# The bias of the hidden layer as three bfloat16 parts, and the loads of early results five tiles later in SyncE's order

## The reference, cut to what matters

```python
logits = xt @ Wr + br                                  # xt: all 8192 tokens
probs, idx = jax.lax.top_k(softmax(logits), 2)         # each token goes to 2 of 8 experts
h = jnp.einsum('td,edf->etf', xt, W1) + b1[:, None, :] # b1: 8 x 512, D=128, F=512
h = _layernorm(relu(h), g1, be1)
y = _layernorm(relu(jnp.einsum('etf,efd->etd', h, W2) + b2[:, None, :]), g2, be2)
x = x + gb * (gate @ y)                                # the two results of a token, weighted
```

## Time and profile before

| | us |
|---|---|
| median of 3 runs | 517.81 (517.48 to 517.86) |
| the profiled execution | 519.68 |
| its span, first to last instruction | 517.6 |
| TensorE busy in the span | 493.6 (95%) |
| VectorE, ScalarE, GpSimd busy | 441.0, 420.0, 365.3 |
| TensorE's granted clock, mean | 0.99 |

### The profile page before, as it was taken

The page is one execution under the profiler, slowest core; times in us unless marked ns, Lnnn a source line. Parts: engine busy times, 40 slices in busy tenths (PEclk is TensorE's granted clock), DMA queues, the critical chain, the costliest instruction groups (busy, mean ns, idle before and its releaser), DMA issues.

```text
span 517.6 us, 14784 instructions
## 1 busy us (share of the span) xinstructions
PE 493.6 (95%) x3101; PEld 393.0 (76%) x3101; DVE 441.0 (85%) x2217; ACT 420.0 (81%) x1148; POOL 365.3 (71%) x483
## 2 busy tenths in 40 slices
PE   7989999999986999999998899999999999999996
PEld 6446665655544799989897789999999989899962
DVE  5778999998887699888887799988989999889893
ACT  5669888978764678888886788899999889999883
POOL 1003666666767778888888878888888888888870
PEclk9999999999997899999999999999999999999999
DMA  6980111145111779867616885666577577667555
GB/s 167 310 233 16 48 47 48 43 134 111 52 46 53 146 166 178 186 200 187 156 52 152 191 224 145 188 198 188 156 200 195 157 193 206 153 184 213 163 164 162
DMA packets 79786, 77.78 MB, mean 150 GB/s; under 512 B 11150, under 2 KB 72745, under 8 KB 79702
## 3 DMA queue, kind: packets, MB, share of 16 engines
q1 hardware_dynamic: 71286, 59.92, 47.4%
q0 software_dynamic: 8416, 16.93, 9.1%
HBM read 54.65 MB, written 22.59 MB: 149 GB/s over the span
## 4 chain that ended last, share of the span: by engine, by line
PE 42%; issue 8%; POOL 6%; DVE 1%; DMA 1%; POOLq 0%; ACT 0%; SPq 0%; DVEq 0%; ACTq 0%
PE bank L1673 15%; PE bank L1570 7%; PE bank L1563 4%; PE bank L1565 4%; PE bank L1564 4%; PE bank L1562 4%; POOL expert_rows L646 3%; PE bank L1554 2%; POOL xi L662 2%; POOL y L662 1%; PE bank L1507 1%; DMA hrow<-expert_rows 1%; PE bank L1686 1%; PE bank L1695 1%; POOL expert_results L674 0%
## 5 line engine op out<-in xcount | busy, mean ns | idle before, releaser
L646 POOL DMA_INDIRECT expert_rows<-rows_ring,slot x128 | 123.1, 962 | 96.1 <-issue 78.6
L674 POOL DMA_INDIRECT expert_results<-y,target x119 | 123.0, 1033 | 31.2 <-issue 26.7
L1673 PE MATMUL bank<-W,h2T 128*128 x720 | 95.5, 276 | 0.8 <-ACT h2T L773 0.3
L1673 PEld LDWEIGHTS bank<-W,h2T 128*128 128x128 f32 x720 | 87.7, 192 | 9.2 <-issue 1.6
L870 ACT ACTIVATE v<-wmod 128x128 f32<-128x128 f32 x135 | 41.9, 311 | 42.3 <-DVE vg L1373 39.2
L1362 DVE SCALAR_TENSOR_TENSOR wmod<-bank,rse,shifts 128x128 f32<-128x128 f32 x119 | 41.6, 350 | 32.9 <-PE bank L1673 25.0
L1562 PE MATMUL bank<-b_parts,onesr 128*128 x135 | 65.1, 482 | 0.7 <-DVE h3lo L1140 0.7
L758 ACT ACTIVATE n<-X,nm,rs 128x128 f32<-128x128 f32 x128 | 54.1, 485 | 8.1 <-DVE nm L1307 8.1
L1145 DVE BATCH_NORM_STATS2 stf<-h1T 128x6 f32<-128x512 f32 x90 | 59.3, 659 | 0.0
L1563 PE MATMUL bank<-W1hi,h3hi 128*128 x135 | 54.1, 401 | 0.0
L1570 PE MATMUL bank<-ident_wr,h1T 128*128 128x128 f32 x360 | 54.0, 273 | 0.0
(11 more groups left out here) (250 smaller groups left out, 1245.7 us busy)
## 6 DMA issues: line engine op xcount, KB each, us to landing
shifts<-expert_shifts SPq DMA_DIRECT2D x119, 192.0 KB, 4.2
hrow<-expert_rows SPq DMA_DIRECT2D x135, 65.0 KB
xi<-expert_results SPq DMA_DIRECT2D x12, 512.0 KB, 6.0
out_x<-X SPq DMA_DIRECT2D x15, 256.0 KB
X<-in_L_attn_x SPq DMA_DIRECT2D x7, 512.0 KB, 7.4
W1lo<-in_L_ffn_W SPq DMA_DIRECT2D x4, 512.0 KB, 6.8
expert_rows<-rows_ring,slot POOLq DMA_INDIRECT x128
expert_results<-y,target POOLq DMA_INDIRECT x119
```

The source lines that it names most:

```text
L646: nc.gpsimd.indirect_dma_start(out=rows_d, out_offset=bass.IndirectOffsetOnAxis(ap=slot[q][:, n // TOPK, n % TOPK:n % TOPK + 1], axis=0), ...
L674: nc.gpsimd.indirect_dma_start(out=results_d, out_offset=bass.IndirectOffsetOnAxis(ap=target[i % TARGETS][:], axis=0), in_=y[k], in_offset ...
L1673: ins = mm(acc, rT[(s - 4) % DEPTH][:, ch * P:(ch + 1) * P], W2[:, bass.ds(e4 * CF + ch, 1), :], start=(ch == 0), stop=(ch == CF - 1))
```

## The change

b1 is split in three bfloat16 parts (`b1_split`), which SyncE copies to the first three rows of a bfloat16 `b1_parts`; the product that adds them takes the bfloat16 `ones` that the kernel has already. The zero filling becomes four copies of the same size, `onesr` goes. ScalarE rounds the first part at the end of its step 0 and the second at the end of its step 1; VectorE subtracts at step 1 as before and once more at step 2. In SyncE's loop, `LOADED_AT` puts `load_early(b)` at i = piece_tile(b, 0) + 6 (59, 66, 74, 82, 89, 97, 105, 113, 120, 128) where it was + 1; batch 10 stays at 131.

```diff
-        b1_parts = sb("b1_parts", [P, E, F], F32R)
-        onesr = sb("onesr", [P, P], F32R)
+        b1_rest = third_rT[0:E, :].bitcast(F32)
+        b1_split = sb("b1_split", [E, 3, F], BF16)
+        b1_parts = sb("b1_parts", [P, E, F], BF16)
...
-            sp.dma_start(b1_parts[0:1, :, :].bitcast(F32), b1hi.bitcast(F32)).then_inc(b1_stored, 16)
-            sp.dma_start(b1_parts[1:2, :, :].bitcast(F32), b1lo[:].bitcast(F32)).then_inc(b1_stored, 16)
+            for n in range(3):
+                sp.dma_start(b1_parts[n:n + 1, :, :], b1_split[:, n, :]).then_inc(b1_stored, 16)
...
-            LOADED_AT = {piece_tile(b, 0) + 1: b for b in range(EARLY)}
+            LOADED_AT = {min(piece_tile(b, 0) + 6, EXPERT_TILES - 4): b for b in range(EARLY)}
...
-            def split_b1():
+            def first_b1_part():
                 act.wait_ge(gains_loaded, 80)
-                act.wait_ge(dve_setup, SETUP_PADDING)
-                nc.scalar.activation(b1hi, b1f[:], ACT.Copy).then_inc(act_setup, 1)
-                nc.scalar.activation(onesr[:], onesf[:], ACT.Copy).then_inc(act_setup, 1)
+                nc.scalar.activation(b1_split[:, 0, :], b1f[:], ACT.Copy).then_inc(act_setup, 1)
+
+            def second_b1_part():
+                act.wait_ge(dve_setup, SETUP_REST)
+                nc.scalar.activation(b1_split[:, 1, :], b1_rest, ACT.Copy).then_inc(act_setup, 1)
...
+            def third_b1_part():
+                dve.wait_ge(act_setup, 4)
+                dve.wait_ge(dve_setup, SETUP_REST)
+                mark(vec.tensor_tensor(b1_split[:, 2, :], b1_rest, b1_split[:, 1, :], ALU.subtract))
...
-                mm(h, onesr[:], b1_parts[:, bass.ds(e, 1), :], start=True, stop=False)
+                mm(h, ones[:], b1_parts[:, bass.ds(e, 1), :], start=True, stop=False)
```

More of the change, by code:

```diff
@@ L117, in adaln_ssm_moe_kernel @@
         third_rT = sb("third_rT", [P, F], F32R)
-        b1hi = third_rT[0:E, :]
-        b1_parts = sb("b1_parts", [P, E, F], F32R)
-        onesr = sb("onesr", [P, P], F32R)
+        b1_rest = third_rT[0:E, :].bitcast(F32)
+        b1_split = sb("b1_split", [E, 3, F], BF16)
+        b1_parts = sb("b1_parts", [P, E, F], BF16)
         onesf = sb("onesf", [P, P])
@@ L143, in adaln_ssm_moe_kernel @@
         b1f = spare_gb[0][0:E, :]
-        b1lo = spare_gb[1][0:E, :]
         assert L == F
@@ L460, in _ @@
             sp.wait_ge(dve_setup, SETUP_END)
-            sp.wait_ge(act_setup, 3)
-            sp.dma_start(b1_parts[0:1, :, :].bitcast(F32), b1hi.bitcast(F32)).then_inc(b1_stored, 16)
-            sp.dma_start(b1_parts[1:2, :, :].bitcast(F32), b1lo[:].bitcast(F32)).then_inc(b1_stored, 16)
+            sp.wait_ge(act_setup, 4)
+            for n in range(3):
+                sp.dma_start(b1_parts[n:n + 1, :, :], b1_split[:, n, :]).then_inc(b1_stored, 16)
             sp.wait_ge(dve_setup, SETUP_PADDING)
@@ L511, in load_shifts @@
                 if i == SLOTS:
-                    sp.wait_ge(b1_stored, 32)
+                    sp.wait_ge(b1_stored, 48)
                 if last_user(i) is not None:
@@ L745, in _ @@
             act.wait_ge(dve_setup, SETUP_PADDING)
-            for e in range(E):
-                ins = nc.scalar.activation(b1_parts[:, e, :], padding[:, TAGS:TAGS + 1].broadcast_to([P, F]), ACT.Copy)
+            for n in range(E // 2):
+                ins = nc.scalar.activation(b1_parts[:, 2 * n:2 * n + 2, :].bitcast(F32).rearrange("p e f -> p (e f)"),
+                                           padding[:, TAGS:TAGS + 1].broadcast_to([P, F]), ACT.Copy)
             ins.then_inc(act_setup, 1)
-            def split_b1():
+            def first_b1_part():
                 act.wait_ge(gains_loaded, 80)
-                act.wait_ge(dve_setup, SETUP_PADDING)
-                nc.scalar.activation(b1hi, b1f[:], ACT.Copy).then_inc(act_setup, 1)
-                nc.scalar.activation(onesr[:], onesf[:], ACT.Copy).then_inc(act_setup, 1)
+                nc.scalar.activation(b1_split[:, 0, :], b1f[:], ACT.Copy).then_inc(act_setup, 1)
+            def second_b1_part():
+                act.wait_ge(dve_setup, SETUP_REST)
+                nc.scalar.activation(b1_split[:, 1, :], b1_rest, ACT.Copy).then_inc(act_setup, 1)
             def normalise(b, dst, x_tiles, rs_, nm_, pieces):
@@ L823, in mixer_step @@
                     normalise(s - 1, n2[1 - q], 0, rs[q], nm[q], range(J // 2, J)).then_inc(n2_ready, 1)
-                if isinstance(s, int) and s == 0:
-                    split_b1()
+                if s == 0:
+                    first_b1_part()
+                if s == 1:
+                    second_b1_part()
             run(mixer_step, FIRST1)
@@ L975, in gains_setup @@
                 dve.wait_ge(act_setup, 3)
-                mark(vec.tensor_tensor(b1lo[:], b1f[:], b1hi, ALU.subtract))
+                mark(vec.tensor_tensor(b1_rest, b1f[:], b1_split[:, 0, :], ALU.subtract))
+                assert done[0] == SETUP_REST
+            def third_b1_part():
+                dve.wait_ge(act_setup, 4)
+                dve.wait_ge(dve_setup, SETUP_REST)
+                mark(vec.tensor_tensor(b1_split[:, 2, :], b1_rest, b1_split[:, 1, :], ALU.subtract))
                 assert done[0] == SETUP_END
@@ L1167, in mixer_step @@
                     gains_setup()
+                if s == 2:
+                    third_b1_part()
                 if on(s - SPLIT_FROM - 1, E):
@@ L1576, in mixer_step @@
                     pe.wait_ge(w1lo_ready, E)
-                    pe.wait_ge(b1_stored, 32)
+                    pe.wait_ge(b1_stored, 48)
                     pe.wait_ge(table_ready, 1)
@@ L1710, in _ @@
                 total_of(b)
-SETUP_PADDING, SETUP_CT, SETUP_MOD, SETUP_GB, SETUP_MIX, SETUP_SUMS, SETUP_END = 2, 3, 4, 8, 12, 13, 14
+SETUP_PADDING, SETUP_CT, SETUP_MOD, SETUP_GB, SETUP_MIX, SETUP_SUMS, SETUP_REST, SETUP_END = 2, 3, 4, 8, 12, 13, 14, 15
 _INS = ['L0_attn_x', 'L0_attn_Win', 'L0_attn_bin_', 'L0_attn_Bp', 'L0_attn_Cp', 'L0_attn_Dp', 'L0_attn_Wout',
```

## The result

The changed kernel takes 590.36 us (median of 4 runs, 588.39 to 593.05), the kernel before beside it 517.64: a ratio of 1.1396, 95% interval 1.1363 to 1.143. The forecast was 590.0. The profiled execution of after took 592.14 with a span of 590.0, against 519.68 and 517.6 before.

The account below looks back on a forecast made before the run. TensorE was taken to bound the second stage. Late loads 55.1, clock 18.0, bias product -1.4 and setup 0.5 sum to +72.2 on 517.81, giving 590.0 us; the forecast's own range was 580 to 597, the wider one 571 to 602.

Parts of the forecast that it names:

- The bound and the late loads: Second stage: TensorE sets the time; loads of batches 0 to 9 come too late and stall it, +55.1 us together.
- a landing of 4 us in the quiet queue: Sign of being wrong: late loads landing in 4 us instead of 6.1, which would take 20 us off.
- behind `h3lo`: Expected sign in the profile after: TensorE waits 5 us behind `h3lo` at the late batches.
- Away goes: Batch 0: SyncE's wait for 39 stored results, which makes tile 55's rows late, disappears; nothing added to the sum.
- The clock: TensorE's granted clock falls behind each of ten stalls, at 1.8 us each: +18.0 us, bounds 0 and 25.5.
- the two rows that the 1.8 was taken from: Two clock falls in the trace before, near 158 and 170 us, costing TensorE 2.55 and 1.7 us.
- Rival 1: TensorE stalls at the late loads but its clock stays up: 572 us; chance 0.10.
- The product with b1: Bias product in bfloat16 is 18 ns shorter over the 79 tiles from 56 on: -1.4 us.
- Rival 4: The bias product gains all of 80 ns, -6.3 us instead of -1.4, on top of the stalls: 585 us; chance 0.05.
- Setup: First stage: an extra copy of half a microsecond on ScalarE before L778 is on the path: +0.5 us (0 to 0.6).
- Rival 2: Stalls feed on each other through slower products, slow landings and costlier clock falls: 601 to 602 us; chance 0.10.
- Rival 3: The moved load is still early enough, so only the other edits count: 516.1 us; chance 0.05.

Follow-up runs that it names:

- run 9: Changed kernel with the relu of the hidden product moved ahead of ScalarE's waiting copy in the ten stalling steps: 588.04 us, ratio 1.1359.
- run 5: Changed kernel with 18 needless TensorE products ahead of the hidden product in the ten stalling tiles, when every kernel was slower: ratio 1.1074.
- run 11: Changed kernel with 18 needless TensorE products ahead of the hidden product in the ten stalling tiles, repeated later: 580.37 us, ratio 1.1187.
- run 3: Changed kernel with load_early at piece + 3 in place of + 6: 519.95 us, ratio 1.0028.
- run 6: Changed kernel, loads still at + 6, with SHIFT_LAG 7 in place of 6 (shifts asked for one tile later in SyncE's order): ratio 1.0791.
- run 1: Kernel before with only the late loads (piece + 6), its bias product left in float32r: 590.24 us, ratio 1.1393.
- run 2: Changed kernel with load_early back at piece + 1, so only the bias edits are left: 517.29 us, ratio 0.9991.
- run 12: The changed kernel itself, run again as a reference beside later runs: 589.4 us, ratio 1.1374.
- run 8: Changed kernel with only batch 5 loaded at piece + 6, all others at + 1: ratio 1.0172; tiles 54 to 134 take 194.95 us.
- run 4: Changed kernel with load_early at piece + 4 in place of + 6: 535.08 us, ratio 1.0331.
- run 7: Changed kernel with load_early back at piece + 1 and SHIFT_LAG 7 in place of 6, when every kernel was slower: ratio 1.0037.
- run 10: Changed kernel with load_early back at piece + 1 and SHIFT_LAG 7 in place of 6, repeated later: 517.17 us, ratio 0.9981.

## Why the prediction was right, step by step

**The bound and the late loads.** Right. The load stands behind the shifts of its own step, goes out 0.39 us behind them (350.51, 350.90), and ScalarE waits at L850 ten times. Of the sum of 55.1, measured 52.7. Two errors in it nearly cancel:
- The landing takes 5.2 us at the median (4.6 to 5.7) instead of 6.1, 9 us less over ten. That the load is quicker because the kernel's other transfers pause in a stall was not tested. The prediction named this as a way to be wrong ("a landing of 4 us in the quiet queue").
- From the copy's start to TensorE it is 1.30 us and not 0.95: the relu behind `h3hi` was missed, +3.5 over ten by the difference, 2.7 by run 9. The sum followed `h3lo` alone. Of the 0.35, 0.27 is the relu (run 9); the other 0.08 is the estimate of signals and issue, which was that much too short. The wait of TensorE "behind `h3lo`" that was to show it reads as one for L772.

The rest, some 3 us, is at batch 0 (8.6 us, forecast 7.3) and at batch 6 (6.7, forecast at most 6.15), where the load took 6.2 us and not 5.2. At batch 0 the load goes out at 301.23, 0.9 later than forecast, which the short landing makes up: the stalled tile starts at 307.35, as forecast. The 1.3 us by which its stall is longer are no loss, since tile 54 starts 1.3 us earlier than before; 0.8 of them are the wait ahead of tile 54, which is gone. That is the point **Away goes** of the prediction, which added nothing, and rightly.

**The clock.** Forecast +18.0, measured 22.0, within the bounds of 0 and 25.5. It fell at all ten places and cost 1.4 to 2.8 us each, 2.2 on average, between the two rows that the 1.8 was taken from. Runs 5 and 11 show that it is TensorE's pause that does it. By the warning of the Trainium skill ("TensorE: Matmul & The Clock Gate", "HAM oscillation") this is paid in every round, and the trace agrees. The mean clock is 0.93 and not the 0.96 that was named as a sign: it is low for part of the pauses too, where it costs nothing. Rival 1 (clock up, 572) is out by this. A rule by the length of the pause alone doesn't come out of the runs: from tile 54 on no pause up to 2.2 us was followed by a fall (1.95 in run 11, 2.09 in run 3, 2.22 in run 6), each from 3.1 us on was, and between them both happened (a fall at 2.35 and 2.44, none at 3.01 and 3.03). The forecast was safe, because its pauses are over 4 us.

**The product with b1.** Forecast -1.4, measured -1.1 (14 ns for each of 80 tiles instead of 18). The row is 379 ns and not 377, and the matching float32r product 395. Rival 4, -6.3, is out: the weight load is half as long (98 ns for 190) and the beat doesn't show it, as the rows have it under the last turn (at tile 95 of after it runs from 438.74 to 438.84, the four turns until 439.01).

**Setup.** Forecast +0.5. Where it arises the forecast is right. From ScalarE's first `xi` (L778 before, L781 now) to that of its step 2 there are 16.90 us in the traces of before and of run 1, which has the old setup, and 17.42 in all twelve with the new one. But in six of these twelve (after and runs 2, 5, 6, 9 and 12) the clock fell right behind, and the next step was 2.1 to 2.2 us late instead of 0.5. In after (windows of 1 us, columns as in the earlier trace rows):

```profile
32.00:33.00 1.00, 0.66 (x5) 0.42 (x4) 0.39 (x1) 1.00 (x3) 0.00 (x0) 0.99 1.15 319
33.00:34.00 1.00, 0.80 (x1) 0.50 (x2) 1.00 (x3) 1.00 (x3) 0.00 (x0) 0.50 1.07 374
34.00:35.00 1.00, 1.00 (x2) 0.34 (x1) 0.90 (x6) 1.00 (x3) 0.00 (x0) 0.50 1.04 382
```

TensorE waits 0.4 us for `xi` there, behind a sparse stretch. Why the clock falls at this place in half of the traces stays open; the sum had no such term. The price went in the waits before tile 54 (4.4 us of them at tiles 46 to 54 before, 0.9 after), so it doesn't reach the end; run 2 as a whole is at 0.9991. In the total the term is near zero.

**Rival 2** (stalls feed on each other, 601) is out by run 8. **Rival 3** (early enough, 516) is what +3 nearly is: the load must go out 5.2 us ahead of the copy, and with +3 it does but for batch 0. The forecast of 590.0 for a measured 590.36 is closer than its terms, and that is luck: stalls -2.4, clock +4.0, bias product +0.3, setup -0.5 and tile 54 earlier by 1.3 add up to +0.1. The mechanism was right, and either of the two larger errors alone would have left the forecast within 4 us.

## What to carry to other kernels

A transfer moved down in a queue costs nothing until its issue plus its landing passes its use by more than the slack, and from there each further step in full, once for each transfer, with the clock's price on top (here 22 us on 53). Look in the trace for which signal holds the instruction ahead of it in its queue: if this signal comes from the step that wants the data, no engine's earliness can save it. When a wait on an in-order engine is lengthened, follow every semaphore behind it, also those that the undisturbed trace never shows as a releaser.

## What the runs showed of the hardware

- The granted clock can fall in a pause and not only at its end: at the ten stalls of after it fell from 4.7 us ahead of TensorE's resume to 0.1 us behind it, and was back 3.0 to 6.0 us after the resume, at a price of 1.4 to 2.8 us.
- The length of the pause alone does not decide. At the late loads the clock fell behind 2.35 us (run 6) and 2.44 (run 4) and stayed full behind 3.01 and 3.03 (run 6); in the sparse first stage a fall stands behind a wait of 0.4 us (33.0 us in after).
- A load of 512 KB landed in 5.2 us at the median into a stalled kernel (4.6 to 5.7 in after) and in 6.1 beside its work (5.6 to 6.5 in before).
- The same chip gave 568.41 us for the kernel before beside runs 5 to 8 and 517.67 later, beside runs 9 to 12. In the two traces of one kernel, runs 7 and 10, the time lies between 60 and 345 us. Single instructions of VectorE, ScalarE and GpSimd had their usual durations (the row store of GpSimd 962 ns and 958), but there was more idle time between them, and TensorE's clock was at half for 55 us ahead of tile 54 where run 10 has 10 (TensorE busy for 510.5 and 492.0 us). What caused it stays open.
